# A two-layer transformer kernel on one core: the second layer's query and key operands stacked to 104 rows, with a masked copy of the keys for each head

## The reference, cut to what matters

```
qkv = grouped_linear(x, w_qkv, None)              # 128 -> 384, 8 groups
qkv = qkv.reshape(B, N, 3, H, D)                  # H = 16 heads, D = 8
q, k, v = (qkv[0] * scale, qkv[1], qkv[2])
attn = jnp.einsum('bhnd,bhmd->bhnm', q, k)        # no mask, 512 x 512 per head
attn = jax.nn.softmax(attn, axis=-1)
out = jnp.einsum('bhnm,bhmd->bhnd', attn, v)
```

## Time and profile before

| what | value |
|---|---|
| three runs | 1146.57, 1147.28, 1134.54 us (median 1146.57) |
| the profiled execution | 1146.85 us, of which the span from first to last instruction is 1145.0 us |
| instructions in the span | 13297 |
| TensorE (PE) busy | 907.2 us, 79% |
| VectorE (DVE) busy | 631.0 us, 55% |
| ScalarE (ACT) busy | 518.3 us, 45% |
| GpSimd (POOL) busy | 190.5 us, 17% |
| mean granted TensorE clock | 0.802 of 2.4 GHz |

### The profile page before, as it was taken

How to read it: one execution, slowest core, us unless ns; L and a number is a source line. 1 busy time by engine, 2 the same in 40 slices (tenths; PEclk the granted TensorE clock), 3 DMA queues, 4 the chain that set the end, 5 groups by cost and what they waited for, 6 DMA issues and landing times. The chain is left out here.

```text
span 1145.0 us, 13297 instructions
## 1 busy us (share of the span) xinstructions
PE 907.2 (79%) x4532; PEld 524.6 (46%) x4532; DVE 631.0 (55%) x1354; ACT 518.3 (45%) x938; POOL 190.5 (17%) x161
## 2 busy tenths in 40 slices
PE   4559999999889999999968689689789961655550
PEld 2325555556557677776732223223323321555540
DVE  3326576866537675675686357577666514322222
ACT  1014545555557767665725345444444430433330
POOL 3625402121010000000022220010010013122215
PEclk9999999999999999999966556756655555766775
DMA  3414111111191000002112600300200000000003
GB/s 109 74 49 121 33 36 29 41 32 29 52 284 36 1 1 1 1 1 37 19 38 53 100 16 10 49 10 10 48 11 1 2 9 28 10 28 28 28 20 81
DMA packets 55647, 44.80 MB, mean 39 GB/s; under 512 B 5831, under 2 KB 46492, under 8 KB 55580
## 3 DMA queue, kind: packets, MB, share of 16 engines
q1 hardware_dynamic: 54555, 41.86, 15.3%
q0 software_dynamic: 1024, 2.10, 0.6%
HBM read 14.71 MB, written 14.55 MB: 26 GB/s over the span
## 5 line engine op out<-in xcount | busy, mean ns | idle before, releaser
L830 ACT ACTIVATE ring<-single 128x512 f32<-128x512 f32 (+3 forms) x512 | 249.9, 516 | 336.6 <-PE single L1031 190.6
L1445 DVE TENSOR_REDUCE mneg<-pair 128x2 f32<-128x1024 f32 (+3 forms) x256 | 259.5, 1022 | 125.0 <-PE pair L1031 66.6
L1031 PE MATMUL single<-q_op,k_op 26*128 26x512 f32 (+3 forms) x512 | 240.8, 570 | 55.0 <-ACT ring L830 31.8
L1031 PE MATMUL pair<-k_op,q_op 24*128 24x512 f32 (+3 forms) x512 | 210.9, 565 | 24.2 <-DVE mneg L1445 17.8
L1031 PEld LDWEIGHTS single<-q_op,k_op 122*128 122x128 f32 (+1 forms) x512 | 105.7, 237 | 168.3 <-ACT ring L830 82.7
L1088 PE MATMUL p_o<-ring,vaug 128*9 128x512 f32 (+3 forms) x1024 | 160.3, 707 | 1.2 <-ACT ring L830 1.2
L1500 DVE TENSOR_TENSOR ring<-ring,single 128x1024 f32<-128x1024 f32 x60 | 73.2, 1221 | 77.5 <-PE single L1143 62.2
L857 ACT ACTIVATE ring<-pair,cols 128x512 f32<-128x512 f32 x136 | 86.0, 685 | 63.9 <-PE pair L1132 62.4
L1031 PEld LDWEIGHTS pair<-k_op,q_op 120*128 120x128 f32 (+1 forms) x512 | 100.5, 246 | 30.8 <-DVE mneg L1445 23.2
L1505 DVE TENSOR_TENSOR hid_lo<-ring,hid_hi 128x1024 fp32r<-128x1024 f32 x68 | 83.2, 1224 | 10.4 <-ACT hid_hi L872 10.3
L872 ACT ACTIVATE hid_hi<-ring 128x1024 fp32r<-128x1024 f32 x68 | 72.1, 1060 | 12.4 <-issue 7.5
(11 more groups left out here) (286 smaller groups left out, 1412.1 us busy)
## 6 DMA issues: line engine op xcount, KB each, us to landing
xs<-zero SPq DMA_DIRECT2D x10, 1024.0 KB, 10.3
q_op<-hl SPq DMA_DIRECT2D x96, 64.0 KB
k_op<-hl SPq DMA_DIRECT2D x96, 64.0 KB
stage<-in_L_ffn_W_dram SPq DMA_DIRECT2D x8, 512.0 KB, 4.4
stage<-in_L_ffn_rW_dram SPq DMA_DIRECT2D x6, 512.0 KB, 5.8
xb<-xs SPq DMA_DIRECT2D x15, 128.0 KB, 2.0
xs<-yb SPq DMA_DIRECT2D x15, 128.0 KB, 1.7
qk_rope<-rope_hl SPq DMA_DIRECT2D x24, 64.0 KB, 2.0
```

Source lines behind the costliest of these rows:

```text
L830: exp_done.by(act.activation(ring[:, n % 8, lo:T], singles[n % 2][:, lo:T], ACT.Exp), (L, n))
L1031: ins = pe.matmul(dst[:, lo:hi], r32(lhs[:, lhs_lo:lhs_lo + P]), r32(rhs[:, lo:hi]), start=True, stop=L == 1)
L1445: s_taken.by(dve.tensor_reduce(mneg[:, G % 2, qt, 2 * p:2 * p + 2], pairs[m % 2][:, :, 0:hi], axis=AX.X, op=ALU.max, negate=True), (L, m))
```

## The change

Layer 2's four heads of a group share one operand of queries, `q_op1` (one tile per group, 104 rows). The rows of the four heads stand above each other: three blocks of 32 rows (head and dimension interleaved), then four rows of maxima, rounded, and four of the rests. The keys are copied in the same form to `k_stk`. From it GpSimd makes, per group, four operands `k_op1`, one per head, by multiplying each row with 1 or 0 (`C_HM`, a new constant), so that only that head's rows are left. `k_op1` has room for 16 heads, four groups. A matmul has 96 rows in a max unit and 104 in an exp unit. The number of matmuls, their columns, and the exponentials, reductions and values stay as they are. The copies are issued by group (6 each) and not by batch (12 for q, 12 for k), and stand at other places of SP's order. The memset of `k_op1` (128 x 4096) becomes one of 32 rows of `k_stk`.

```diff
-            def head1_dma(a_, w):
-                taken.wait_ge(sp, (("q", "k")[w], a_))
-                if a_ >= NB + 2:
-                    exp_done.wait_ge(sp, (1, 64 * (a_ - NB - 1) - 1))
-                elif w == 0:
+            def head1_dma(G):
+                r, g = G // NG, G % NG
+                if G >= NG:
+                    exp_done.wait_ge(sp, (1, 16 * (G - NG) + 15))
+                elif G == 0:
                     sp.wait_ge(k_ones, 1)
                     apart(sp)
-                for j in range(GH):
+                for w, part in enumerate(("q", "k")):
+                    taken.wait_ge(sp, (part, NB + r))
                     for t in range(3):
-                        sp.dma_start((q_op1, k_op1)[w][32 * j + HD * t:32 * j + HD * (t + 1), a_ % 2, :, :],
-                                     hl[32 * j:32 * j + 32, 2 * w + TERM[w][t], :]).then_inc(head_rows1[a_ % 2], 16)
+                        sp.dma_start((q_op1, k_stk)[w][32 * t:32 * (t + 1), g, :],
+                                     hl[32 * g:32 * g + 32, 2 * w + TERM[w][t], :]).then_inc(head_rows1[g], 16)
...
-                        dst = q_op1[24 + part:P:32, G // NG % 2, G % NG, :]
+                        dst = q_op1[96 + GH * part:96 + GH * (part + 1), G % NG, :]
...
-                if r < NB - 1:
-                    head1_dma(NB + r + 1, 0)
                 m_dma(1, G + 2)
                 if r < NB - 1:
-                    head1_dma(NB + r + 1, 1)
+                    head1_dma(G + 4)
...
                 if r < NB - 1:
+                    head1_dma(G + 5)
                     m_dma(1, G + 4)
+                    head1_dma(G + 6)
+                    head1_dma(G + 7)
...
-            pool.memset(k_op1[:, :, :, :], 1.0).then_inc(k_ones, 1)
+            pool.memset(k_stk[96:P, :, :], 1.0).then_inc(k_ones, 1)
+            pool.wait_ge(k_ones, 1)
...
+            def mask(G):
+                g = G % NG
+                pool.wait_ge(head_rows1[g], H_ROWS * (G // NG + 1))
+                if G >= 4:
+                    exp_done.wait_ge(pool, (1, 16 * (G - 4) + 15))
+                elif G == 2:
+                    y_step.wait_ge(pool, units[-1])
+                apart(pool)
+                for j in range(GH):
+                    ins = pool.tensor_scalar(r32(k_op1[0:104, GH * ((G + 2) % 4) + j, :]), k_stk[0:104, g, :],
+                                             cst[0:104, C_HM + j:C_HM + j + 1], None, ALU.mult)
+                k_masked.by(ins, G)
+
+            for G in range(3):
+                mask(G)
             for s in range(NB, STAGES):
+                G = NG * (s - NB)
                 add_bias(s)
+                mask(G + 3)
                 if s == NB:
-                    for n in range(len(PIECE1)):
+                    for n in range(0, 4):
                         weights1(n)
                 else:
                     modulate(s - 1)
+                if s < STAGES - 1:
+                    mask(G + 4)
+                if s == NB:
+                    for n in range(4, 6):
+                        weights1(n)
+                if s < STAGES - 1:
+                    mask(G + 5)
+                if s == NB:
+                    for n in range(6, len(PIECE1)):
+                        weights1(n)
+                else:
                     scatter(s - 1)
+                if s < STAGES - 1:
+                    mask(G + 6)
...
-                        act.wait_ge(head_rows1[(s - 1) % 2], H1_ROWS * ((s - 1 - NB) // 2 + 1))
+                        for g in range(NG):
+                            act.wait_ge(head_rows1[g], H_ROWS * (s - NB))
...
-                return tuple(op[32 * j:32 * j + K, G // NG % 2, G % NG, :] for op in (q_op1, k_op1))
+                rows_in = 96 if K == 24 else 104
+                return q_op1[0:rows_in, G % NG, :], k_op1[0:rows_in, GH * ((G + 2) % 4) + j, :]
...
-                    elif G % NG == 0:
-                        pe.wait_ge(head_rows1[G // NG % 2], H1_ROWS * (G // (2 * NG) + 1))
+                    else:
+                        k_masked.wait_ge(pe, G)
```

More of the change, by code:

```diff
@@ L38 @@
 C_IOTA = C_LT + E1 * E1
+C_HM = C_IOTA + 16
 NBLK = T * NB // 256 + E1 - 1
-C_N = C_IOTA + 16
+C_N = C_HM + GH
 B_MS, B_MT, B_TRI, B_ONE = 0, P, 2 * P, 3 * P
@@ L73, in constants @@
     c[:, C_IOTA:C_IOTA + 16] = np.arange(16)
+    for j in range(GH):
+        c[:, C_HM + j] = ((p < 96) & (p % GH == j)) | (p == 96 + j) | (p == 96 + GH + j)
     b = c[:, C_N:]
@@ L317, in build @@
         hid_lo = put("hid_lo", [P, 2, 2, T], at=at_op + 8 * KB)
-        q_op1 = put("q_op1", [P, 2, NG, T], at=at_op + 16 * KB)
-        k_op1 = put("k_op1", [P, 2, NG, T], at=at_op + 32 * KB)
+        k_op1 = put("k_op1", [P, 4 * GH, T], at=at_op)
+        q_op1 = put("q_op1", [P, NG, T], at=at_op + 32 * KB)
+        k_stk = put("k_stk", [P, NG, T], at=at_op + 40 * KB)
         xb = put("xb", [P, 3, 2, D], at=at_op)
@@ L392, in build @@
         head_rows = [sem(f"head_rows{s}") for s in range(3)]
-        head_rows1 = [sem(f"head_rows1_{s}") for s in range(2)]
+        head_rows1 = [sem(f"head_rows1_{g}") for g in range(NG)]
+        k_masked = sig("k_masked", list(range(4 * NG)))
         rope_rows = sem("rope_rows")
@@ L423, in build, with by_head, by_dim @@
         acc = [p_o, p_m, p_o, p_m]
-        M_ROWS, H_ROWS, H1_ROWS, R_ROWS = 32, 16 * 6, 16 * 24, 16 * 6
+        M_ROWS, H_ROWS, R_ROWS = 32, 16 * 6, 16 * 6
         TERM = [(0, 0, 1), (0, 1, 0)]
-        PERM = [lambda ap: ap.rearrange("p (g j d) -> p g d j", g=NG, j=GH), lambda ap: ap.rearrange("p (g j d) -> p j d g", g=NG, j=GH)]
-        PERMED = [lambda ap: ap.rearrange("p (g d j) -> p g d j", g=NG, d=HD), lambda ap: ap.rearrange("p (j d g) -> p j d g", j=GH, d=HD)]
+        def by_head(ap):
+            return ap.rearrange("p (g j d) -> p g d j", g=NG, j=GH)
+        def by_dim(ap):
+            return ap.rearrange("p (g d j) -> p g d j", g=NG, d=HD)
         @block.sync
@@ L573, in _ @@
                              zero[:, :].unsqueeze(1).broadcast_to([P, 16, D])).then_inc(zeroed, 16)
-            head1_dma(NB, 0)
-            head1_dma(NB, 1)
+            for g in range(NG):
+                head1_dma(g)
             expert1(0)
@@ L627, in _ @@
             half = DR // 2
-            pool.tensor_copy(PERMED[0](rhs_abs[:, 0:P]), PERM[0](raw[:, 2 * P:3 * P]))
+            pool.tensor_copy(by_dim(rhs_abs[:, 0:P]), by_head(raw[:, 2 * P:3 * P]))
             pool.tensor_copy(rhs_abs[:, 2 * P + DR:2 * P + DR + half], rhs_abs[:, 2 * P + half:2 * P + DR])
             pool.tensor_copy(rhs_abs[:, 2 * P + DR + half:2 * P + 2 * DR], rhs_abs[:, 2 * P:2 * P + half]).then_inc(pool_set, 1)
-            pool.tensor_scalar(PERMED[0](w_q[0][:, :]), PERM[0](raw[:, 0:P]), SCALE0, None, ALU.mult)
+            pool.tensor_scalar(by_dim(w_q[0][:, :]), by_head(raw[:, 0:P]), SCALE0, None, ALU.mult)
             pool.tensor_copy(w_rope[:, DR:DR + half], w_rope[:, half:DR])
@@ L681, in _ @@
             pool.wait_ge(loads[4], n_load[4])
-            pool.tensor_scalar(PERMED[1](w_q[1][:, :]), PERM[1](w_qkv[:, 0:D]), SCALE1, None, ALU.mult)
-            pool.tensor_copy(PERMED[1](w_k1[:, :]), PERM[1](w_qkv[:, D:2 * D]))
+            pool.tensor_scalar(by_dim(w_q[1][:, :]), by_head(w_qkv[:, 0:D]), SCALE1, None, ALU.mult)
+            pool.tensor_copy(by_dim(w_k1[:, :]), by_head(w_qkv[:, D:2 * D]))
             pool.wait_ge(cols_ready, 1)
```

## The result

**1069.6 us** is the median of three runs (1067.49 to 1072.36), against 1146.57 before: ratio 0.9361, 95% interval 0.9261 to 0.9462. The forecast was 1062, with a range of 1038 to 1100. The profiled execution took 1072.36 us, with a span of 1070.6 and a mean clock of 0.916 (before 0.802). Some executions of one kernel come out over 1.5% above its fastest, as two of four in experiment 4 and one of two in experiment 2 did; all times are then given, and the shorter ones are compared.

The account below looks back on a forecast made before the run. TensorE, busy but at a granted clock of 0.58 in layer 2's attention, was taken as the bound. 63 quads at 4.0 us make 252 in place of 337 us, 85 less: 1146.85 - 85 = 1062 us, range 1038 to 1100.

Parts of the forecast that it names:

- rival A: Layer 2's attention: more rows in use bring the full clock; 1062 us, 1038 to 1085, chance 0.72.
- rival B: Layer 2's attention: clock stays at 1.2 GHz and the heads lose concurrency; 1189 us, chance 0.09.
- The doubt about zeros: Masked keys in layer 2's scores: no row showed whether an array fed three quarters zeros still gets the full clock.
- Rival D: Layer 2's attention: clock rises but falls back in plain quads, half the gain; about 1125 us, chance 0.07.
- Terms 1, 3 and 4: Layer 2's plain quad at full clock: eight scores 1.83 us, values 0.98 in place of 1.82, quad taken as 3.1.
- Term 2: Layer 2's scores: heads no longer run side by side, costing 0.5 us per quad at equal clock, 32 us in all.
- Term 5: Layer 2's quads with other parts: 4.3 us for twelve per stage, 3.1 for four, so 4.0 us on average.
- Term 6: SP's copies: maxima ahead of head copies remove the 19.6 us stall, counted inside the 4.0 us per quad.
- The cover of 4 us: Masked keys for group G + 4: ready in 8 us, two quads, against a deadline three quads off.
- Rival C: Masked keys come late, holding PE in three groups of three stages, 36 us; 1098 us, chance 0.12.
- Term 7: GpSimd's 64 masks: 0.52 us each, 2.1 per group (at most 5.1), 33 us in all, hidden under other work.
- Term 8: Small items at nothing: shrunken memset, ScalarE's waits, the lead's twelve max units held by VectorE, the drain.

Follow-up runs that it names:

- experiment 4: Kernel before plus an overwritten 128-row matmul ahead of each exp unit's scores, four per quad: 1165.35, 1174.94, 1192.4 and 1197.96 us.
- experiment 2: The changed kernel with layer 2's score matmuls cut to the first 64 rows: two times, 1125.66 and 1157.76 us.
- experiment 9: Change run again, 1069.47 us; change with two first-stage expert loads moved behind the fifth group's keys, 1063.71; masks made by copies with that move, 1062.84.
- experiment 1: The changed kernel with layer 2's score matmuls cut to the first 32 rows, all else kept: 1179.72 us, ratio 1.0307.
- experiment 5: The changed kernel without GpSimd's 64 masks, all heads of a group reading the stacked keys at 96 and 104 rows: 1053.16 us, ratio 0.9184.
- experiment 3: The kernel before with only SP's order changed, maxima of group G + 2 ahead of q's twelve copies: 1142.57 us, ratio 0.999.
- experiment 6: The changed kernel with GpSimd's masks multiplying by the constant 1.0 instead of a per-partition value: 1065.34 us, ratio 0.9339.
- experiment 7: The changed kernel with a group's four masks made by one two-tensor GpSimd multiply with broadcast operands: 1081.46 us, ratio 0.9475.

## Why the prediction was right

The mechanism, rows for clock, was right: 85 us forecast, 77 measured. The sum came out near in part by luck, since its wrong terms stood on both sides. By the profiled execution the forecast missed 10.4 us (1072.4 against 1062). The attention gives 9.1 of it (261.1 against 252), the time up to the first values 3.3, and the end gives 1.8 back. Of the 9.1, 2.5 are this execution's own: near its end the clock fell once more, to 0.55 and 0.71 in two quads of 4.88 and 4.19 us, which take 3.47 and 3.08 in the second profile of the change (experiment 9), whose attention takes 257.8 us.

**The clock, rival A against B.** Shown, from three sides. With 104 rows 0.96, forecast 0.95 or more; with 32 rows and all else equal 0.61, and 0.50 in plain quads (experiment 1); with full-height matmuls added and nothing else changed up to 1.00 (experiment 4). The doubt about zeros is settled by experiment 5, for 104 rows. Experiment 1, the nearest to rival B, took 1179.7 us where B was priced at 1189. Rival D did not come: plain quads stay up.

**Terms 1, 3 and 4.** Values take the 0.98 us forecast (660.00 to 660.97). Two scores of 96 rows back to back run from 661.31 to 661.77, 0.23 each. A plain quad is 3.39 us against 3.1; the waits between score batches are longer than I took, 2.42 us for eight matmuls of 1.83. That is 0.3 us on four quads of each of the four stages, some 5 us.

**Term 2, what packing is worth, was too large.** It charged every quad 0.5 us at an equal clock. The one quad that the forecast built on took 3.93 us before, from 622.27 to 626.20; the same quad of the change, from 618.58 to 622.52, takes 3.94, not 4.4. Fifteen quads stood at a clock of 1.00 throughout in the kernel before (four) and in experiment 3 (eleven). Without masks (experiment 5) the same quads take from 0.19 us less to 0.37 us more, 0.1 on average. What holds these quads in place of the scores is open.

**Term 5, loaded quads.** 4.14 us over all quads against 4.0. Without masks it is 3.88, below the forecast. By stage, without masks, it is 3.98, 4.04, 4.03 and, in the last, 3.46 us. The first three confirm 4.0, though for a mixed reason: the quad of 3.93 was a light one, and the 0.5 us added to it did not come. The last stage has no next batch's parts beside it, and the forecast gave it 4.0 all the same; its 15 quads are 8 us shorter than that, which hid half of what the masks cost.

**Term 6, SP's order.** The stall of 19.6 us went, as forecast. But I gave this to the order of the copies, and experiment 3 shows that the order alone brings nothing. The cover of 4 us for the keys was eaten in the first stage, where the expert loads stand ahead of the fifth group's copies. Rival C had both this place and the mechanism, at 36 us; it came at 9.0, and 5.8 are what the long wait was worth (experiment 9).

**Term 7, the masks, is the term that was mis-sized most:** 0.52 us each forecast, at most 1.28, and 1.576 measured, 99.9 us of GpSimd and not 33. I took the copy as nearest and the multiply of two tensors as the bound from above; the form is dearer than either, and no row of before showed it. Experiment 6 rules out its operand as the reason. My statement that work alone hides the masks was wrong in a second way: GpSimd's instructions lengthen VectorE's, which I didn't consider at all. VectorE's busy time rose by 7.4 us over before (638.4 against 631.0), 8.9 over the same kernel without masks. The cost in time: 16 to 17.5 us in all, 5.8 by the fifth group's keys. Where the rest stands, a comparison quad by quad shows, between the second profile of the change and the kernel without masks: in the last three stages twelve quads are 0.2 to 1.6 us longer, 9.5 us together, and the other 35 are equal within 0.06. PE's waits for masks there are some 3 us of this (8.6 in all, of which 5.5 in the first stage's long one). That VectorE's 8.9 us make up what is left is argued from their size; no run separates the two.

**Term 8, the lead.** I had put it at nothing, since VectorE holds its max units, and the first values came 3.3 us later. Of this 0.5 came from ahead of the lead, whose first matmul starts at 578.04 and not at 577.53. The lead itself takes 21.5 us (before 18.8). From 584 us on its clock is 0.50 in both kernels. Two max units take 2.54 us together, from 583.98 to 586.52, where before one took 1.14 (585.73 to 586.87); the first exp unit comes 16.1 us into the lead in place of 14.6. From the first exp unit to the first values it takes 5.42 us against 4.16. So in the lead the change pays for its lost concurrency and has no higher clock for it:

```profile
583.98 2.37 PE L1074 MATMUL pair<-k_op,q_op 96*128 96x512 f32 x4 [0.17 <-DVE mneg L1489]
```
```profile
585.73 0.79 PE L1031 MATMUL pair<-k_op,q_op 24*128 24x512 f32 x2 [0.34 <-DVE mneg L1445]
```

Without masks (experiment 5) the lead takes 20.7 us, from 581.84 to 602.55; so the masks are 0.8 us of it, where I had expected 2. Whether PE or VectorE ends last between the max units stays open.

## What to carry to other kernels

When TensorE is busy and slow, read rows in use beside the granted clock: packing short contractions side by side was worth 0.1 us per quad at an equal clock, and left the kernel at half the clock for most of its quads. Put nothing on GpSimd at the price of a neighbouring form, and count what it does to VectorE's short instructions, even where GpSimd itself has time to spare. A wait for a copy that is cured by moving one entry of a queue is cured only if what it passes has as much slack; shorten the blocks first, then order them.

## What the runs showed of the hardware

- GpSimd multiplies 104x512 elements by a scalar in 1.50 to 1.58 us, longer than it multiplies or adds two tensors of 128x512 (1.28), and three times half of what a 1024-element cast takes (1.037). One multiply of 104x2048 with broadcast operands takes 3.67 us, 0.92 per 512.
- A VectorE instruction of 0.16 us stood for 2.76 us beside a GpSimd instruction of 3.60, until that ended (experiment 7).
- At the full clock a score matmul of 26 rows starts 0.31 to 0.33 us behind the full-height one ahead of it (experiment 4, four in the quad shown), where two of 96 rows start 0.23 apart (the change, 661.31).
- With 64 rows in use the clock stood at 0.50 and at 0.88 in neighbouring stretches of the same loop (experiment 2, the longer execution).
- With 32 rows in use the clock stood at 0.50 while PE was busy all of 50 us (experiment 1, 850 to 900).
